# A decoder layer on one core: projection tiles between transposes, two rank products a chunk, and six of eight key tiles added on GpSimd

## The reference

```python
x = x + self_attention(layernorm(x))            # 16 heads of 32, causal
x = x + cross_attention(layernorm(x), context)  # softmax(Q K^T / sqrt(32)) V, then out @ W_o + b_o
x = x + moe(layernorm(x))

# inside moe: xf is the normalised input, 4096 tokens
gate_scores = xf @ gate_W + gate_b                       # 4 experts
topk_scores, topk_idx = top_k(gate_scores, 2)
weights = softmax(topk_scores)
expert(e) = layernorm(relu(layernorm(xf @ W1[e] + b1[e])) @ W2[e] + b2[e])   # with gains and shifts
moe = sum over the two experts of weight * expert(xf) + xf
```

## Time and profile before

| What | us |
|---|---|
| median of 3 runs | 4533.93 (4533.02 to 4535.35) |
| the profiled execution | 4499.94 |
| its span, first to last instruction | 4498.2 |
| TensorE busy in the span | 4079.3 (91%) |
| VectorE busy | 2722.7 (61%) |
| ScalarE busy | 2096.6 (47%) |
| GpSimd busy | 2476.6 (55%) |
| mean granted TensorE clock | 0.935 of full speed |

### The profile page before, as it was taken

The page is one execution under the profiler, slowest core; times in us unless marked ns, Lnnn a source line. Parts: engine busy times, 40 slices in busy tenths (PEclk is TensorE's granted clock), DMA queues, the critical chain, the costliest instruction groups (busy, mean ns, idle before and its releaser), DMA issues. The chain is left out here.

```text
span 4498.2 us, 61641 instructions
## 1 busy us (share of the span) xinstructions
PE 4079.3 (91%) x21970; PEld 2522.1 (56%) x21970; DVE 2722.7 (61%) x4947; ACT 2096.6 (47%) x3870; POOL 2476.6 (55%) x931
## 2 busy tenths in 40 slices
PE   6998999997788998999999999999999967549997
PEld 5874555554667886444444444444444346438886
DVE  4436777773453334777777777777777333326765
ACT  2112555554122110566666666666666533226665
POOL 0002334332000001799999999999999915518887
PEclk8996999998899997999999999999999977669998
DMA  4546453522555556022222222222222056134444
GB/s 145 177 155 147 100 109 86 112 47 87 206 189 181 178 171 169 23 57 57 57 58 57 58 58 57 57 58 58 57 57 57 6 189 122 38 99 81 80 83 63
DMA packets 275065, 432.72 MB, mean 96 GB/s; under 512 B 31689, under 2 KB 132041, under 8 KB 268618
## 3 DMA queue, kind: packets, MB, share of 16 engines
q1 hardware_dynamic: 251050, 390.23, 32.6%
q0 software_dynamic: 19776, 36.85, 4.8%
q10 hardware_dynamic: 3968, 2.10, 0.2%
HBM read 258.57 MB, written 170.52 MB: 95 GB/s over the span
## 5 line engine op out<-in xcount | busy, mean ns | idle before, releaser
L881 DVE TENSOR_REDUCE cross_neg_max<-cross_scores 128x1 f32<-128x512 f32 x2048 | 1264.7, 676 | 397.0 <-PE cross_scores L708 396.9
L665 POOL TENSOR_TENSOR cross_partial<-cross_partial,cross_probs 128x2048 f32<-128x2048 f32 x320 | 1465.6, 4580 | 66.7 <-ACT cross_probs L832 29.5
L832 ACT ACTIVATE cross_probs<-cross_shifted 128x512 f32<-128x512 f32 x2048 | 1074.1, 606 | 748.0 <-PE cross_shifted L720 713.8
L708 PE MATMUL cross_scores<-cross_k_stack,cross_q_stack 96*128 96x512 f32 x2048 | 875.6, 437 | 39.5 <-DVE cross_neg_max L881 27.5
L720 PE MATMUL cross_shifted<-cross_q_stack,cross_k_stack 98*128 98x512 f32 x2048 | 850.7, 420 | 15.2 <-DMA cross_q_stack<-cross_neg_dram 6.7
L720 PEld LDWEIGHTS cross_shifted<-cross_q_stack,cross_k_stack 98*128 98x128 f32 x2048 | 387.1, 190 | 388.6 <-issue 239.9
L708 PEld LDWEIGHTS cross_scores<-cross_k_stack,cross_q_stack 96*128 96x128 f32 x2048 | 395.1, 193 | 286.6 <-DVE cross_neg_max L881 224.4
L832 ACT ACTIVATE self_probs<-self_shifted 128x512 f32<-128x512 f32 (+3 forms) x768 | 358.5, 492 | 366.2 <-PE self_shifted L723 285.3
L881 DVE TENSOR_REDUCE self_neg_max<-self_scores 128x1 f32<-128x512 f32 (+3 forms) x768 | 388.2, 547 | 207.1 <-PE self_scores L708 109.5
L736 PE MATMUL cross_out<-cross_probs,cross_v 128*32 128x512 f32 x4096 | 497.2, 603 | 0.0
L708 PE MATMUL self_scores<-self_k_stack,self_q_stack 96*128 96x512 f32 (+3 forms) x768 | 308.6, 423 | 21.7 <-DMA self_k_stack<-k_hi 10.0
(11 more groups left out here) (271 smaller groups left out, 6241.5 us busy)
## 6 DMA issues: line engine op xcount, KB each, us to landing
cross_k_stack<-k_hi SPq DMA_DIRECT2D x30, 1024.0 KB, 20.4
kv_x_in<-in_ctx SPq DMA_DIRECT2D x16, 1024.0 KB, 5.5
k_hi<-kv_out_hi SPq DMA_DIRECT2D x64, 256.0 KB, 2.6
k_lo<-kv_out_lo SPq DMA_DIRECT2D x64, 256.0 KB, 3.2
v<-kv_out_n SPq DMA_DIRECT2D x64, 256.0 KB, 2.3
cross_v<-v SPq DMA_DIRECT2D x32, 512.0 KB, 25.1
self_q_stack<-q_hi SPq DMA_DIRECT2D x30, 512.0 KB, 6.9
self_k_stack<-k_hi SPq DMA_DIRECT2D x30, 512.0 KB, 15.6
```

The costliest lines, as they stand in the source:

```text
L665: nc.gpsimd.tensor_tensor(total, total, own, ALU.add).then_inc(pool_added.sem, 1)
L708: mm = nc.tensor.matmul(scores[at][:, 0:width], q_st[0:96, w, h, q0:q0 + P], k_st[0:96, w, h, half * WIDE:half * WIDE + width], start=True ...
L832: nc.scalar.activation(probs[:, e % NE % PB, h, f:], shifted[n % SHIFTED][:, f:], ACT.Exp).then_inc(exped.sem, 1)
L881: nc.vector.tensor_reduce(neg_max[:, q % 2, column(a), half:half + 1], scores[n % (SLOTS * ROUNDS) % AHEAD][:, 0:width], AX.X, ALU.max, ne ...
```

## The change

It has two parts that don't touch each other.

In `attend`, for a block with eight key tiles (only self attention has one), GpSimd adds the tiles 0, 1, 2, 4, 5, 6 instead of 0, 1, 4, 5. The cross attention's list is not changed.

In `finish`:
- Three of the four projection tiles of chunk c+2 are issued right behind the transposes of tiles 1, 2 and 3 of chunk c, the fourth stays behind the gate products. VectorE's additions move in the same way: tiles 0 to 2 stand behind its low parts 1 to 3, and so ahead of `scales`; tile 3 stays.
- The high part of the next attention chunk moves on ScalarE from the start of pass c+1 to pass c, behind `g_rows` and the weight; its low part on VectorE moves into `gate(c)`, in front of the second half.
- `counted` holds the counts before each tile instead of before each chunk. VectorE fills it with four linked additions a chunk in place of one reduction and one addition. Rank is then two products of 16 columns for all four tiles.

```diff
-        return {4: (), 8: (0, 1, 4, 5), 16: (0, 1, 2, 3, 4, 5, 8, 9, 10, 11, 12, 13)}[sets_of(qb)]
+        return {4: (), 8: (0, 1, 2, 4, 5, 6), 16: (0, 1, 2, 3, 4, 5, 8, 9, 10, 11, 12, 13)}[sets_of(qb)]
...
-        counted = sb("counted", [P, CHUNKS + 1, EXPERTS])
+        counted = sb("counted", [P, TILES + 1, EXPERTS])
...
+            attention_high(2)
             for c in range(CHUNKS):
-                if c + 2 < CHUNKS:
-                    attention_high(c + 2)
...
                 if c % 2 == 0:
                     weight_high(c // 2)
+                if c + 3 < CHUNKS:
+                    attention_high(c + 3)
                 act.wait_ge(less_max, c + 1)
...
+                nc.vector.tensor_tensor(offset[:, :, :], taken[:, here, :], per_tile(from_end[:, here]), ALU.mult)
+                for t in range(c * TPC, (c + 1) * TPC):
+                    link(nc.vector.tensor_tensor(counted[:, t + 1, :], counted[:, t, :], taken[:, t, :], ALU.add))
                 dve.sem_inc(masked, 1)
-                nc.vector.tensor_tensor(offset[:, :, :], taken[:, here, :], per_tile(from_end[:, here]), ALU.mult)
-                link(nc.vector.tensor_reduce(in_chunk[:, :], taken[:, here, :].rearrange("p t e -> p e t"), AX.X, ALU.add))
-                nc.vector.tensor_tensor(counted[:, c + 1, :], counted[:, c, :], in_chunk[:, :], ALU.add)
+                if c + 3 < CHUNKS:
+                    attention_low(c + 3)
                 dve.wait_ge(exped, c + 1)
...
                     if t == 0 and c + 1 < CHUNKS:
                         variance(c + 1)
+                    if t and c + 2 < CHUNKS:
+                        add_projection(c + 2, t - 1)
                 if c + 1 < CHUNKS:
                     scales(c + 1)
...
                 if c + 2 < CHUNKS:
-                    add_projection(c + 2)
+                    add_projection(c + 2, TPC - 1)
                 gate(c)
...
-                for t in range(TPC):
-                    mm = nc.tensor.matmul(rank_ps[:, t, :], before[:, :], taken[:, c * TPC + t, :], start=True, stop=False, skip_group_check=True)
-                    for other in range(t):
-                        mm = nc.tensor.matmul(rank_ps[:, t, :], all_ones[:, :], taken[:, c * TPC + other, :], start=False, stop=False, skip_group_check=True)
-                    mm = nc.tensor.matmul(rank_ps[:, t, :], all_ones[:, :], counted[:, c, :], start=False, stop=True, skip_group_check=True)
-                mm.then_inc(ranked, 1)
+                here = slice(c * TPC, (c + 1) * TPC)
+                nc.tensor.matmul(rank_ps[:, :, :], before[:, :], taken[:, here, :], start=True, stop=False)
+                nc.tensor.matmul(rank_ps[:, :, :], all_ones[:, :], counted[:, here, :], start=False, stop=True).then_inc(ranked, 1)
...
                 for t in range(TPC):
-                    pe.wait_ge(normed, TPC * c + t + 1)
-                    after(pe, lo_ready, TPC * c + t - 1)
-                    for k in range(KT):
-                        mm = nc.tensor.transpose(turned[t % 2][:, k, :], x_n[:, u, t, k * P:(k + 1) * P], ident[:, :])
-                    mm.then_inc(turned_ready, 1)
+                    turn_tile(c, t)
+                    if t and c + 2 < CHUNKS:
+                        project_tile(c + 2, t - 1)
                 if c:
                     rank_tokens(c - 1)
...
                 if c + 2 < CHUNKS:
-                    project_tokens(c + 2)
+                    project_tile(c + 2, TPC - 1)
```

More of the change, by code:

```diff
@@ L1417, in _ @@
             dve.wait_ge(made, 15)
-            add_projection(0)
+            for t in range(TPC):
+                add_projection(0, t)
             attention_low(1)
@@ L1421, in _ @@
             scales(0)
-            add_projection(1)
+            for t in range(TPC):
+                add_projection(1, t)
+            attention_low(2)
             for c in range(CHUNKS):
-                if c + 2 < CHUNKS:
-                    attention_low(c + 2)
                 for t in range(TPC):
@@ new lines, in rank_tokens, with project_tile @@
+                nc.tensor.matmul(rank_ps[:, :, :], before[:, :], taken[:, here, :], start=True, stop=False)
+                nc.tensor.matmul(rank_ps[:, :, :], all_ones[:, :], counted[:, here, :], start=False, stop=True).then_inc(ranked, 1)
+            def project_tile(c, t):
+                if t == 0:
+                    pe.wait_ge(a_lo_ready, c + 1)
+                after(pe, added, TPC * c + t - 1)
+                i = 0
+                for part, w in ((a_hi, ow_hi), (a_hi, ow_lo), (a_lo, ow_hi)):
+                    for k in range(KT):
+                        nc.tensor.matmul(acc[t % 2][:, :], part[:, k, t * P:(t + 1) * P], w[:, k, :], start=i == 0, stop=False)
+                        i += 1
+                nc.tensor.matmul(acc[t % 2][:, :], first_row[:, :], bias_hi[:, :], start=False, stop=False)
+                nc.tensor.matmul(acc[t % 2][:, :], first_row[:, :], bias_lo[:, :], start=False, stop=True).then_inc(acc_ready, 1)
@@ L1468, in _, with turn_tile @@
+            def turn_tile(c, t):
+                pe.wait_ge(normed, TPC * c + t + 1)
+                after(pe, lo_ready, TPC * c + t - 1)
+                for k in range(KT):
+                    mm = nc.tensor.transpose(turned[t % 2][:, k, :], x_n[:, c % 2, t, k * P:(k + 1) * P], ident[:, :])
+                mm.then_inc(turned_ready, 1)
             pe.wait_ge(ow_lo_ready, 1)
@@ L1499, in _ @@
             pe.wait_ge(weighed, CHUNKS)
[L1500 removed]
+            nc.tensor.matmul(count_ps[:, :], all_ones[:, :], counted[:, TILES, :], start=True, stop=True).then_inc(counts_ready, 1)
 def experts(nc, w2, vectors, xn, lists, w1_hi, w1_lo, table, valid, out, ident):
```

28 lines of the change are left out of this document (7 added, 21 removed).

## The result

The changed kernel takes **4452.3 us** (median of 4 runs, 4446.99 to 4454.07) against 4533.5 (4 runs, 4530.22 to 4535.35): ratio 0.982, 95% interval 0.9803 to 0.9837, 81 us less. The profiled execution took 4446.99 us, span 4445.3. Against the profiled execution of before that is only 53 us less, and I had written 4444 for it.

A forecast was written before the change was run, and what follows sets the result against it. TensorE was taken to bound self attention, a loop of waits between engines to bound finish. Gains of 18 and 38 us, together 56, came off the median 4533.93: 4478 us, range 4458 to 4503.

The forecast's parts named there:

- 4444: Whole kernel: the time in us forecast for a profiled execution, from 4499.94 less 56.
- finish walk: Finish stage: one steady chunk followed step by step across the engines, 27.1 us against 34.8; stage gain 38 us.
- the stage's tail: End of finish: from scatter 5 on GpSimd runs through, before and after; scatter 5 starts at 3837 instead of 3875.31.
- the steady rounds: Self attention: each round but the last saves TensorE 1.38 us, counted 15 times, with no wait on GpSimd.
- the last round: End of self attention: GpSimd's adds become the path, 20.8 us, so 2.5 us are given back.
- Rival 3: Self attention gains nothing because adds come over 1.15 us late each round; gain 38, 4496 us, chance 0.08.
- I take off the same 56: Whole kernel: the gain of 18 + 38 us, worked out on the profiled execution, subtracted unchanged from the median 4533.93.
- the 34 us: Whole kernel: the median's excess over the profiled execution, 4533.93 against 4499.94, left in place by the forecast.
- The clock: Finish: TensorE's clock falls in a 4.9 us pause, so projection tile 0 takes 5.7 us, later ones about 3.2.
- the two long issues: Finish, GpSimd: one or two scatter issues a chunk take about 2.97 us beside VectorE's two-input SBUF subtractions.
- Rival 1: Finish: the clock doesn't fall before tile 0 and GpSimd's scatters set a 24.9 us period; 4466 us, chance 0.13.

The follow-up runs named there:

- The kernel with one pause: The changed kernel with one short GpSimd operation, waited for, behind the eighth of a chunk's sixteen scatters: 4450.5 us, ratio 0.9820 to the kernel before.
- rank early: The changed kernel with the rank of the chunk before moved behind the first projection tile: 4453.0 us, ratio 0.9824 to the kernel before.

## Why the prediction was wrong in its number and right in most of its steps

- **The finish walk held.** Tile 0 was to start 6.0 us behind the gate transposes: 5.6 and 5.9 measured (3694.65 to 3700.23, 3722.02 to 3727.95). Its length at the low clock: 5.7 foreseen, 5.9. The next tile with its transposes: 3.7 foreseen, 3.66 (3734.23 to 3737.89). Rank 0.85 foreseen, 0.36, as its products ran at the high clock. Scatter start 20.9 foreseen, 21.2 (3715.83). The chunk: 27.1 foreseen, 26.7. The root was free 1.8 us before `scales` wanted it (3713.47 against 3715.23); I had said 1. From its first projection to the end of its last scatter the stage took 283.5 us instead of 320.3: 36.8 gained, 38 foreseen. That this is so near is in part luck. Scatter 5 stands 41.5 us earlier against the start of the stage, not 38, and the stage's tail, which I had GpSimd run through, is 4.7 us longer than before, with pauses of 5.5 and 6.1 us in it where before had one of 6.5.
- **Self attention: the steady rounds held, the end was mis-sized.** The rounds fell to 41.65 us, and up to the fourteenth partial sum 20.0 us were gained (3.0 of them stand at the first one already, where a round gives 1.3). I had the last round give back 2.5 us; the last two gave back 7.2 (the last scale stands at 1067.33, 12.8 us earlier). The adds themselves take 21.1 us, 20.8 foreseen. What I missed is the round before the last: it is short too (38.18 us before, with 24 products of scores instead of 48), and TensorE waits 2.18 us there; and the last round's first add begins only 16.5 us earlier than before, where I left its place relative to the rest unchanged. Timed alone, this half gives 13.5 us, 18 foreseen. Rival 3 (waits in each round) did not happen.
- **The failed step is the last: "I take off the same 56".** It assumed that the 34 us between the profiled execution and the median lay outside what the change touches. They lay in the very loop that it reorders: late reports in five of eight chunks. The interleaving leaves no row of 56 projection products (the expectations say 64, with the eight transposes behind them) beside a run of sixteen scatters, and in the changed kernel's additions only a few reports are late, the longest by 3.2 us. So finish gained 36.8 + 36.8 us in usual executions (73.4 in the run with this half alone), and the medians of the changed kernel (4446 to 4452) are 2 to 8 us above the 4444 written for the profiled execution, with nothing of the 34 us added. Had I taken the 34 us as a term of its own, with all of it lost or kept, the range would have reached 4444.
- **Late reports are left in the tail.** In the last loop pass of the changed kernel no projection is left and one run of scatters goes beside it. TensorE's transposes of the first two tiles, then ScalarE's second high part:

```profile
3825.31 1.97 PE L1474 MATMUL finish_turned<-ident,finish_x_n 128*128 128x128 f32 x8
...
3838.30 0.60 ACT L1300 ACTIVATE finish_xt_hi<-finish_turned 128x512 fp32r<-128x512 f32 x1 [7.75 <-issue]
```

  The transposes are recorded as done at 3827.28, 11.0 us before. The third tile, the rank behind it and the next scatter wait for this, and it is the 5.5 us pause of GpSimd named above. The kernel with one pause has no such wait (its last pass takes 13.6 us, not 25.1), and the same time: its pauses cost GpSimd as much.
- **The clock and the two long issues.** Both went as written: 0.50 in tile 0 and 1.00 behind it, and a scatter issue of 2.71 us at 3726.02 beside VectorE's subtraction of two SBUF operands that begins at 3725.60, as one of 2.98 us at 3688.47 beside a subtraction that begins at 3688.08. The Trainium skill's page "SBUF — State Buffer" (section "SBUF: two separate sides") has the two shut each other out for a whole instruction; the trace agrees again. Rival 1's other half, GpSimd as the bound, was near enough for me to believe in it afterwards; the kernel without scatters in the loop refuted it.

## What to carry to other kernels

Before a change is priced from one profiled execution, compare that execution's own time with the median: where they differ, the difference sits in some stage, and if the change touches that stage it is a term of the sum, not an offset. A wait whose named releaser was long done is worth a look at who is active through it; here it was the engine that nobody waited for. On a kernel that scatters from GpSimd beside short TensorE groups, a pause in the run of issues may be worth more than the issue time it costs, and gains from closing up TensorE's products are to be tried with it.

## What the runs showed of the hardware that I had not expected

- What TensorE reports to other engines came late while GpSimd issued indirect DMAs 1.265 us apart without a break. With runs of sixteen an addition began up to 10.2 us behind the end of the last recorded product (rank early), and in the changed kernel's last pass a high part of ScalarE 11.0 us behind the transposes (13.1 in its second profile). With a run of 112 it was 87 us. With an operation of 1 us, waited for, behind every fourth issue no engine waited more than 1 us for a report (two kernels). With one behind the eighth the waits were up to 2.9 us (three kernels). With the scatters out of the loop no report in it was late until the run began in the last pass (three kernels).
- In the two places shown with runs of sixteen the report came 2.6 and 2.7 us behind the end of the last issue, but others came while the run went on, and the one of the run of 112 came 9.5 us behind it. So no run here gives a rule for when it comes.
- It is not in every execution: one of before, 34 us quicker than all others seen, had none with the same runs of issues. Why, stays open, and so does what is late. In the place shown TensorE's products are recorded on their usual pitch and its clock fell to 0.50 meanwhile, which speaks for the semaphores alone; beside the run of 112 the products themselves stood 2.80 us apart.
- The granted clock fell to 0.50 in every pause in front of a projection tile in the changed kernel's loop (five, of 4.2 to 4.5 us), and was back at 1.00 when that tile ended, 4.8 to 6.1 us later.
